# Decoder layer on one core: the softmax's division by its sum as a scaled copy on ScalarE instead of a product on VectorE

## The chip, the cores and the metric

The kernel runs on 1 core of one Trainium2 chip. The metric is the device time of one execution in microseconds (us); less is better. The core has five engines that run side by side and wait for one another through semaphores: TensorE (PE in the profile, its weight loads PEld), VectorE (DVE), ScalarE (ACT), GpSimd (POOL) and SyncE (SP, which issues the transfers).

## The reference

One decoder layer in float32 on x (8, 256, 128) and a context of the same shape. Each of its three parts adds its result to its input and normalises:

```python
x = _layernorm(x + attention(x, ...))
x = _layernorm(x + retention(x, ctx, ctx))
x = _layernorm(x + experts(x, ...))
```

The change touches the attention alone. For each query, an indexer picks 96 keys (the last 64, and 32 others that it rates highest); keys and values come from a latent of 32 numbers, with 8 heads:

```python
scores = (einsum("bhld,bhlkd->bhlk", q_c, k_c) + einsum("bhld,blkd->bhlk", q_r, key_r)) * scale
attn = softmax(scores, axis=-1)
out = einsum("bhlk,bhlkd->bhld", attn, v)
```

The softmax is exp(score - maximum), divided by the sum of these over the keys of a query and head. The retention part multiplies decayed scores with the context; the experts part takes the best two of 8 experts for every token.

## The kernel before

The program is one list of instructions for each engine, all written by one function `program`, so that every engine meets the pieces in the same order. The outer loop is over steps (one batch of 256 tokens starts its attention in each of the steps 0 to 7), the inner one over 20 slots of a step. Four strands of different batches are interleaved in a slot: `stage_a` (projections and the indexer's top keys, for the next batch), `stage_b` (attention, for this batch), `stage_c` (retention, for the batch before) and `stage_d` (router, two batches back). From step 2 on, `tile` adds the experts of earlier batches: four products with weights, four copies with a ReLU on ScalarE (`ht`, line 1581), four more products. The last third of a step's slots has no attention tile. After step 8 come the dense experts, without attention.

`stage_b` handles one tile of 16 tokens x 8 heads = 128 rows in each of the slots 0 to 15, 128 tiles in all. The first four tiles of a batch see 96 keys (the narrow form, 128x96), the other twelve see 96 near keys and 4 x 32 columns of gathered far ones (the wide form, 128x224). For tile t:

- PE, slot t: `scores` writes bank bS (lines 1088, 1091, 1094); `gather` fetches the far latents of the next tile into bG (line 1075).
- DVE, slot t: the maximum of a row, negated, into `nmx` (line 1808 narrow, line 1813 wide, where the scores also go to `pp`); then `gs` from bG (line 1820).
- ACT, slot t: `pp = exp(...)` with the sum of a row into `lsum` (line 1495, two instructions: the exponential and the read of the sum). At quarter past the slot it waits for PE's `turn` of the tile before and copies out `pts` (1505, 1507), `vgs` (1509), `ots` (1516).
- DVE, three quarters past: `rls = 1/lsum` (line 1798), then `ppn = pp * rls` (line 1801).
- PE, a quarter past slot t+1: `turn` transposes `ppn` into bank bM (line 919); in slot t+2 `weigh` multiplies it with the latents (lines 1117, 1122).

`pp`, `ppn`, `lsum`, `rls` and `nmx` have two buffers, by the parity of t. Signals count per tile: `s_exp` (exponential done), `s_rec` (reciprocal done), `s_nrm` (`ppn` written), `m_full` (bM filled), `m_out` (bM copied out). Three places wait for `s_nrm`: PE's `turn`, ACT's exponential and DVE's wide maximum, the last two for the tile two before theirs (their buffer of `pp`).

The order of the pieces within a slot, for every engine, is: stage_a, stage_c, stage_b at s; stage_d; the first half of an expert tile; stage_b at s+0.25; stage_a, stage_c, stage_d at s+0.5; stage_b at s+0.75; the second half of an expert tile.

Other lines that the prediction names: `sm` (line 1883, DVE, the retention's decayed scores, from PE's bC of line 1227), `qV` (line 1549, ACT, four copies scaled by a number of each partition), `kS` (line 1535, ACT, the same shape without that scale), `rb`, `pa`, `pr`, `ka` (stage_a's work on ACT), `oh` (line 1788), `xt` and `ot` (lines 2012, 2018, DVE, experts), the tile list (lines 1973 to 2000, DVE, once in each of three steps), `sorted_tokens` and `gb` (lines 863 and 851, POOL's indirect transfers), `taken` (line 1963, DVE, router).

Of the kernel before, what the change touches and what calls it, by code (L numbers as in the profile page):

```python
# [19 lines left out]
ALU = mybir.AluOpType  # L20
ACT = mybir.ActivationFunctionType
# [14 lines left out]
NT = L // TQ  # L36
# [186 lines left out]
def build(nc, io, out):  # L223
    ctx = ExitStack()
    with ctx:
# [1147 lines left out]

        @block.scalar
        def _(act):
            for s_ in (a_free, a_soft, own_aa, s_exp, m_out, c_freeA, c_ret, ln_rs, own_ac, r_ex, own_ad, f_rs):
                act.sem_inc(s_.sem, s_.per * s_.lead)
            AC = nc.scalar.activation
            copy = nc.scalar.copy
# [105 lines left out]
            def stage_b(s, i):  # L1485
                p = i.par
                if s < 0:
                    return
                if s == int(s):
                    if s < NT:  # L1490

                        act.wait_ge(s_max.sem, s_max.at(i.n, s + 1))
                        act.wait_ge(s_nrm.sem, s_nrm.at(i.n, s - 1))
                        w = 96 if s < T0 else SW
                        AC(pp[:, s % 2, 0:w], bS[:, 0:w] if s < T0 else pp[:, s % 2, :], ACT.Exp, scale=1.0 if s < T0 else -1.0,  # L1495
                           bias=nmx[:, s % 2:s % 2 + 1], accum_out=lsum[:, s % 2:s % 2 + 1]).then_inc(s_exp.sem, 1)
                    return
                if s > int(s) + 0.25:
                    return
                s = int(s)  # L1500
                if 1 <= s <= NT + 1:

                    act.wait_ge(m_full.sem, m_full.at(i.n, s))
                    if s <= T0:
                        last = copy(pts[0:96, 0:128], bM[0:96, 0:128])
                    elif s <= NT:
                        last = copy(pts[:, :], bM[:, 0:256])  # L1507
                    if T0 < s <= NT:
                        last = copy(vgs[:, :].rearrange("p (c l) -> p c l", c=4),
                                    bM[:, LATENT:LATENT + 128].rearrange("p (l c) -> p c l", c=4))  # L1510
                    if 2 <= s:
                        t = s - 2
                        if t == 0:

                            act.wait_ge(c_full.sem, c_full.at(i.n - 1, C_AT["out"] + 1))
                        last = copy(ots[:, :, TQ * t:TQ * t + TQ], bM[:, WEIGHED:WEIGHED + 32].rearrange("p (a q) -> p a q", a=2))
                    last.then_inc(m_out.sem, 1)
# [103 lines left out]

        @block.vector
        def _(dve):
            for s_ in (own_va, g_top, r_ks, r_qs, top_a, top_b, a_slot, o_ready, g_out, s_max, s_rec, s_nrm, c_freeV, ln_st, own_vc,
                       c_x1, c_x2, r_lg, r_m, r_place, own_vd, own_vf, f_st, ln_root):
                dve.sem_inc(s_.sem, s_.per * s_.lead)
            TT, TS, STT = nc.vector.tensor_tensor, nc.vector.tensor_scalar, nc.vector.scalar_tensor_tensor
# [147 lines left out]
            def stage_b(s, i):  # L1775
# [17 lines left out]
                if s == int(s) + 0.75 and s < NT:  # L1793

                    t = int(s)
                    w = 96 if t < T0 else SW
                    dve.wait_ge(s_exp.sem, s_exp.at(i.n, t + 1))
                    nc.vector.reciprocal(rls[:, t % 2:t % 2 + 1], lsum[:, t % 2:t % 2 + 1]).then_inc(s_rec.sem, 1)
                    dve.wait_ge(m_full.sem, m_full.at(i.n, max(0, t - 1)))
                    dve.wait_ge(s_rec.sem, s_rec.at(i.n, t + 1))  # L1800
                    TS(ppn[:, t % 2, 0:w], pp[:, t % 2, 0:w], rls[:, t % 2:t % 2 + 1], None,  # L1801
                       ALU.mult).then_inc(s_nrm.sem, 1)
                if s != int(s):
                    return
                if s < NT:
# [303 lines left out]
```

## Time and profile before

| | |
|---|---|
| median of 3 runs | 690.98 us (687.41 to 692.0) |
| the profiled execution | 683.81 us, its span 682.0 us |
| mean granted clock of TensorE | 0.906 |
| busy: PE, DVE, ACT, POOL | 578.3, 479.7, 362.2, 268.4 us |
| attention tiles | 128 (96 wide, 32 narrow), between 39 and 570 us |
| first maximum of the 8 batches, at | 39.6, 100.3, 163.2, 227.1, 297.7, 368.3, 446.6, 515.4 us |

The profile is of one execution, which was some 7 us under the median of the timed ones. Its instructions overlap: a DVE or ACT instruction often starts before the one ahead of it has ended, so that what an instruction costs its engine is the distance between starts, less than its duration. Idle time is put down to whoever released the engine last.

### The profile page before, as it was taken

The page shows a single profiled execution, that of the slowest core. Times are in us where ns is not written, and L with a number is a line of the kernel's source. Part 1 is how long each engine was busy: PE and PEld are TensorE (multiplying, and loading weights), DVE is VectorE, ACT ScalarE, POOL GpSimd, SP SyncE. Part 2 cuts the span into 40 slices and gives each one's busy share as a digit, 9 for nine tenths or more (in the row PEclk, how much of TensorE's full clock was granted, in tenths as well). Part 3 has the DMA queues.
Part 4 walks back from the last instruction along what each step waited for, and adds up shares of the span by engine and source line. Part 5 has one row for each costly group of instructions (what it writes and reads, how often), then busy time and mean ns, then how long its engine had stood idle before and what let it go on. Part 6 is the DMA issues. An engine that isn't in the chain of part 4 may idle for free.

```text
span 682.0 us, 22130 instructions
## 1 busy us (share of the span) xinstructions
PE 578.3 (85%) x8149; PEld 441.2 (65%) x8149; DVE 479.7 (70%) x1746; ACT 362.2 (53%) x1253; POOL 268.4 (39%) x428
## 2 busy tenths in 40 slices
PE   5379977996898789989997788979996998789996
PEld 4255654664566456776786566757885677678886
DVE  1948848986986798569965896679767685434653
ACT  4344545563655446637764554566654444554352
POOL 1415812911570287014801698418403563104310
PEclk9657797898899769989998799799998897999999
DMA  5030163113013142463335143543362524686551
GB/s 166 13 110 17 23 194 122 22 33 111 13 23 112 27 134 54 149 198 98 108 111 160 44 145 84 162 150 110 98 198 79 176 76 111 199 236 197 178 164 42
DMA packets 58594, 75.85 MB, mean 111 GB/s; under 512 B 14256, under 2 KB 47480, under 8 KB 57336
## 3 DMA queue, kind: packets, MB, share of 16 engines
q1 hardware_dynamic: 56952, 71.30, 35.1%
q0 software_dynamic: 1536, 3.15, 1.6%
q8 instruction: 65, 1.06, 0.7%
q14 instruction: 41, 0.34, 0.2%
HBM read 58.92 MB, written 8.62 MB: 99 GB/s over the span
## 4 chain that ended last, share of the span: by engine, by line
PE 31%; DVE 10%; POOL 10%; issue 8%; ACT 6%; DMA 1%; SPq 0%; DVEq 0%; POOLq 0%; ACTq 0%
PE bW L1352 4%; PE bH L1287 3%; PE bR L1302 3%; PE bG L1075 3%; POOL gb L851 3%; PE bM L919 2%; ACT qV L1549 2%; PE bH L1338 2%; PE bG L1338 2%; PE bS L1094 2%; PE bM L1122 1%; PE bM L1117 1%; ACT ht L1581 1%; POOL sorted_tokens L863 1%; PE bC L1227 1%
## 5 line engine op out<-in xcount | busy, mean ns | idle before, releaser
L1495 ACT ACTIVATE pp<-pp,nmx 128x224 f32<-128x224 f32 x96 | 46.5, 485 | 98.3 <-DVE nmx L1813 98.2
L1820 DVE TENSOR_TENSOR gs<-bG,rank_t 96x512 f32<-96x512 f32 x96 | 65.4, 681 | 11.8 <-PE bG L1075 11.6
L809 POOL TENSOR_TENSOR r<-x,cst 128x256 f32<-128x256 f32 x8 | 5.8, 726 | 145.3 <-DVE x L1847 145.3
L1075 PE MATMUL bG<-oh,kspl 128*96 128x512 f32 x160 | 59.4, 454 | 0.0
L1801 DVE TENSOR_SCALAR ppn<-pp,rls 128x224 f32<-128x224 f32 (+1 forms) x128 | 48.8, 382 | 14.5 <-PE bM L919 0.5
L1581 ACT ACTIVATE ht<-bH,wt 128x128 f32<-128x128 f32 x156 | 44.7, 375 | 22.1 <-PE bH L1287 22.1
L1883 DVE TENSOR_TENSOR sm<-bC,cst 128x512 f32<-128x512 f32 x64 | 43.4, 679 | 15.2 <-PE bC L1227 15.0
L919 PE MATMUL bM<-cst,ppn 128*128 128x128 f32 (+1 forms) x224 | 51.1, 300 | 3.2 <-DVE ppn L1801 3.2
L1227 PE MATMUL bC<-qV,kS 128*128 128x512 f32 x64 | 34.6, 540 | 17.3 <-DVE sm L1883 11.8
L1507 ACT COPY pts<-bM 128x256 f32<-128x256 f32 x96 | 35.0, 365 | 25.8 <-PE bM L919 25.3
L1302 PE MATMUL bR<-wt,ht 128*128 128x128 f32 x264 | 40.0, 300 | 9.4 <-DVE taken L1963 9.3
L1122 PE MATMUL bM<-pts,vgs 128*32 128x8 f32 x3072 | 46.7, 182 | 0.0
L1117 PEld LDWEIGHTS bM<-pts,ckw 96*32 96x32 f32 x1024 | 21.0, 112 | 38.9 <-issue 38.2
L1287 PE MATMUL bH<-xt,wt 128*128 128x128 f32 x312 | 44.5, 289 | 1.8 <-DVE xt L2012 1.8
L1302 PEld LDWEIGHTS bR<-wt,ht 128*128 128x128 f32 x264 | 37.0, 211 | 13.4 <-issue 11.0
L1094 PE MATMUL bS<-gs,qall 96*32 96x128 f32 x768 | 43.3, 300 | 2.0
L1091 PE MATMUL bS<-kd,qall 128*128 128x96 f32 x192 | 39.7, 291 | 6.1 <-DVE nmx L1813 6.0
L851 POOL DMA_INDIRECT gb<-expert_rows,slot x24 | 26.5, 1104 | 46.7 <-DMA expert_rows<-ot 40.2
L1813 DVE CUSTOM_DVE_ANT_0 pp<-bS,cst 128x224 f32<-128x224 f32 x96 | 36.3, 378 | 11.0 <-PE bS L1094 10.9
L1287 PEld LDWEIGHTS bH<-xt,wt 128*128 128x128 f32 x312 | 41.1, 203 | 2.6 <-DVE xt L2012 2.2
L1122 PEld LDWEIGHTS bM<-pts,vgs 128*32 128x32 f32 x3072 | 42.7, 119 | 0.0
L1091 PEld LDWEIGHTS bS<-kd,qall 128*128 128x128 f32 x192 | 33.8, 207 | 13.0 <-DVE nmx L1813 9.2
(294 smaller groups left out, 1583.8 us busy)
## 6 DMA issues: line engine op xcount, KB each, us to landing
wt<-in_experts SPq DMA_DIRECT2D x61, 578.0 KB, 4.1
sidx<-far_slots SPq DMA_DIRECT2D x8, 1536.0 KB, 6.8
vstk<-gs SPq DMA_DIRECT2D x96, 64.0 KB
xs<-sorted_tokens SPq DMA_DIRECT2D x45, 64.0 KB, 3.9
expert_rows<-ot SPq DMA_DIRECT2D x45, 64.0 KB, 3.6
sorted_tokens<-acc SPq DMA_DIRECT2D x9, 256.0 KB, 2.9
cst<-shape_constants SPq DMA_DIRECT2D x1, 1595.5 KB, 6.4
xn<-in_x SPq DMA_DIRECT2D x8, 128.0 KB, 3.2
```

The lines of the kernel that those rows point to most:

```text
L851: nc.gpsimd.indirect_dma_start(gb[:, n % NG, 2 * k + t, :], None, ys_dram[g][:, :], bass.IndirectOffsetOnAxis(ap=slot[:, n, 2 * k + t:2 * ...
L919: return MM(dst, src, ident[lo:lo + n, lo:lo + n], is_transpose=True, start=True, stop=True)
L1075: last = MM(w[0:96, :], table, oh[:, pair % 2, kt, SLOTS * (tile % 2):SLOTS * (tile % 2) + SLOTS], start=(n == 0), stop=(n == len(products ...
L1091: MM(bS[:, o:o + 96], q, kd[:, p, k0:k0 + 96], start=True, stop=True, skip_group_check=True)
L1094: last = MM(bS[32 * c:32 * c + 32, o + 96:o + SW], qall[0:96, p, 128 * tile + 32 * c:128 * tile + 32 * c + 32], gs[:, g % 2, 128 * c:128 * ...
L1122: last = MM(bM[32 * j:32 * j + 32, WEIGHED:WEIGHED + 32].rearrange("p (a q) -> p a q", a=2)[:, :, 4 * c:4 * c + 4], vgs[:, 32 * c:32 * c + ...
L1287: last = MM(w[:, 128 * f:128 * f + 128], wt[:, t % NW, 128 * f:128 * f + 128], xt[:, t % 2, :], start=True, stop=True)
L1302: last = MM(w[:, 0:128], ht[:, t % 2, f, :], wt[:, t % NW, W2_AT + 128 * f:W2_AT + 128 * f + 128], start=(f == 0), stop=(f == 3))
L1495: AC(pp[:, s % 2, 0:w], bS[:, 0:w] if s < T0 else pp[:, s % 2, :], ACT.Exp, scale=1.0 if s < T0 else -1.0, bias=nmx[:, s % 2:s % 2 + 1], a ...
L1581: last = AC(ht[:, t % 2, f, :], w[:, 128 * f:128 * f + 128], ACT.Relu, bias=wt[:, t % NW, FF + f:FF + f + 1])
L1801: TS(ppn[:, t % 2, 0:w], pp[:, t % 2, 0:w], rls[:, t % 2:t % 2 + 1], None, ALU.mult).then_inc(s_nrm.sem, 1)
L1820: TT(gs[:, g % 2, :].rearrange("p (t j) -> p t j", j=FAR), bG[0:96, :].rearrange("p (t j) -> p t j", j=FAR), rank_t[:, :].rearrange("p (o ...
```

## The change

The product `ppn = pp * rls` leaves VectorE. ScalarE computes it as a copy with the scale `rls` (one number for each partition), at s+0.75, which in ScalarE's order is behind its copies of the slot and behind what `stage_a` and `stage_c` do at s+0.5, and ahead of the experts' ReLU copies. The reciprocal stays on VectorE, and ScalarE waits for its signal `s_rec`. VectorE's own waits for `s_rec` and for `m_full` go away; ScalarE has waited for a later count of `m_full` at s+0.25.

```diff
@@ scalar engine, stage_b @@
+                if s == int(s) + 0.75 and s < NT:
+
+                    t = int(s)
+                    w = 96 if t < T0 else SW
+                    act.wait_ge(s_rec.sem, s_rec.at(i.n, t + 1))
+                    AC(ppn[:, t % 2, 0:w], pp[:, t % 2, 0:w], ACT.Copy, scale=rls[:, t % 2:t % 2 + 1]).then_inc(s_nrm.sem, 1)
@@ vector engine, stage_b @@
                     t = int(s)
-                    w = 96 if t < T0 else SW
                     dve.wait_ge(s_exp.sem, s_exp.at(i.n, t + 1))
                     nc.vector.reciprocal(rls[:, t % 2:t % 2 + 1], lsum[:, t % 2:t % 2 + 1]).then_inc(s_rec.sem, 1)
-                    dve.wait_ge(m_full.sem, m_full.at(i.n, max(0, t - 1)))
-                    dve.wait_ge(s_rec.sem, s_rec.at(i.n, t + 1))
-                    TS(ppn[:, t % 2, 0:w], pp[:, t % 2, 0:w], rls[:, t % 2:t % 2 + 1], None,
-                       ALU.mult).then_inc(s_nrm.sem, 1)
```

The two lists of signals that each engine raises once at its start are changed to match: `s_nrm` moves from VectorE's to ScalarE's.

## Rows read from the trace of the kernel before

**Rows 1.** The page: busy time; TensorE's clock in 40 slices (10 is full).
```profile
PE 578.3 (85%) x8149; PEld 441.2 (65%) x8149; DVE 479.7 (70%) x1746; ACT 362.2 (53%) x1253; POOL 268.4 (39%) x428
PEclk9657797898899769989998799799998897999999
```

**Rows 2.** Waits: engine, line, releaser, us in total, times, longest us.
```profile
ACT pp L1495 <- DVE nmx L1813: 98.2, 70, 3.3
ACT pp L1495 <- DVE nmx L1808: 39.7, 23, 3.0
...
PE bC L1227 <- DVE sm L1883: 11.8, 7, 3.4
...
PE bS L1091 <- DVE nmx L1813: 6.0, 8, 2.6
```

**Rows 3.** Lines by form: costs of removed, added and neighbouring instructions.
```profile
L1801 DVE TENSOR_SCALAR ppn<-pp,rls 128x224 f32<-128x224 f32 x96 | 38.1, 397 | 11.0 <-PE bM L919 0.5 <-DVE rls L1798 0.5
...
L1801 DVE TENSOR_SCALAR ppn<-pp,rls 128x96 f32<-128x96 f32 x32 | 10.7, 336 | 3.5
...
L1495 ACT ACTIVATE pp<-pp,nmx 128x224 f32<-128x224 f32 x96 | 46.5, 485 | 98.3 <-DVE nmx L1813 98.2
...
L1549 ACT ACTIVATE qV<-bC,cst 128x512 fp32r<-128x512 f32 x64 | 38.7, 691 | 2.1 <-PE bC L919 1.9
...
L1535 ACT CAST kS<-bC 128x512 fp32r<-128x512 f32 x16 | 9.6, 598 | 3.2 <-PE bC L919 3.2
```

**Rows 4.** Timeline of DVE in two slots of the third batch: start, duration.
```profile
179.42 0.16 DVE L1798 RECIPROCAL rls<-lsum 128x1 f32<-128x1 f32 x1
179.69 0.53 DVE L1801 TENSOR_SCALAR ppn<-pp,rls 128x224 f32<-128x224 f32 x1
180.13 0.08 DVE L1742 MATCH_VALUE_LOAD ia<-va,sa 128x8 f32 x1
...
183.41 0.15 DVE L1798 RECIPROCAL rls<-lsum 128x1 f32<-128x1 f32 x1
183.66 0.34 DVE L1801 TENSOR_SCALAR ppn<-pp,rls 128x224 f32<-128x224 f32 x1
183.92 0.29 DVE L1740 MAX8 va<-sa 128x8 f32<-128x128 f32 x1
```

**Rows 5.** Timeline of ACT, third and fifth batch.
```profile
163.44 0.34 ACT L1495 ACTIVATE pp<-bS,nmx 128x96 f32<-128x96 f32 x1 [1.50 <-DVE nmx L1808]
163.68 0.19 ACT L1495 ACTIVATION_READ_ACCUMULATOR pp<-bS,nmx 128x1 f32 x1
...
309.64 1.14 ACT L1581 ACTIVATE ht<-bH,wt 128x128 f32<-128x128 f32 x4
...
315.25 0.48 ACT L1495 ACTIVATE pp<-pp,nmx 128x224 f32<-128x224 f32 x1
315.64 0.19 ACT L1495 ACTIVATION_READ_ACCUMULATOR pp<-pp,nmx 128x1 f32 x1
```

**Rows 6.** Timeline of PE, third batch: idle before and releaser in brackets.
```profile
181.97 0.59 PE L1227 MATMUL bC<-qV,kS 128*128 128x512 f32 x1 [1.00 <-DVE sm L1883]
...
194.86 0.46 PE L1091 MATMUL bS<-kd,qall 128*128 128x96 f32 x2 [0.35 <-DVE nmx L1813]
...
201.05 0.44 PE L919 MATMUL bM<-cst,ppn 128*128 128x128 f32 x2 [0.91 <-DVE ppn L1801]
```

**Rows 7.** Chain that ended last, fourth batch: start, us, what.
```profile
231.90 0.27 DVE ppn L1801
...
258.33 0.69 DVE sm L1883
...
266.50 0.36 DVE ppn L1801
266.91 0.44 PE bM L919 x2
```

**Rows 8.** Windows of the fifth batch: busy us and instructions by engine.
```profile
core 0: us, PE busy (x) PEld busy (x) DVE busy (x) ACT busy (x) POOL busy (x), PEclk, DMA share, GB/s
...
327.00:357.00 30.00, 29.86 (x566) 23.98 (x567) 24.20 (x81) 18.61 (x65) 11.61 (x19) 1.00 0.40 111
```

**Rows 9.** Chain that ended last, sixth batch and start of the eighth.
```profile
379.24 1.03 POOL sorted_tokens L863
...
423.17 0.73 POOL acc L885
...
533.79 4.30 DMA expert_rows<-ot
```

More of the change, by code:

```diff
@@ L1375, in _ @@
         def _(act):
-            for s_ in (a_free, a_soft, own_aa, s_exp, m_out, c_freeA, c_ret, ln_rs, own_ac, r_ex, own_ad, f_rs):
+            for s_ in (a_free, a_soft, own_aa, s_exp, s_nrm, m_out, c_freeA, c_ret, ln_rs, own_ac, r_ex, own_ad, f_rs):
                 act.sem_inc(s_.sem, s_.per * s_.lead)
@@ L1623, in _ @@
         def _(dve):
-            for s_ in (own_va, g_top, r_ks, r_qs, top_a, top_b, a_slot, o_ready, g_out, s_max, s_rec, s_nrm, c_freeV, ln_st, own_vc,
+            for s_ in (own_va, g_top, r_ks, r_qs, top_a, top_b, a_slot, o_ready, g_out, s_max, s_rec, c_freeV, ln_st, own_vc,
                        c_x1, c_x2, r_lg, r_m, r_place, own_vd, own_vf, f_st, ln_root):
```

## The prediction

> **What bounds the kernel now.** I read the page's busy times first [rows 1]. TensorE leads with 85%, VectorE has 70%, ScalarE 53%. The row of clocks shows that the first half of the attention runs partly at half clock. No engine is full over the whole span, so a share tells little. The reader should ask of every stretch which engine sets the pace.
>
> The list of waits came next [rows 2]. ScalarE's exponential waits for VectorE's maximum in 70 of the 96 wide tiles and in 23 of the 32 narrow ones, 137.9 us in all, 1.5 us each time. ScalarE is normally ahead and VectorE late. But TensorE waits little for VectorE: 11.8 us for `sm`, 6.0 us for the maximum. These two, with single waits for `ppn`, are what a quicker VectorE can give back during the tiles.
>
> The chain that ended last and the timelines then tell how a batch goes. It has three kinds of stretch. In some VectorE is the pace (around 181, 195 and 200 us [rows 6], around 231 and from 258 to 266 us [rows 7]). In some ScalarE has no pause (309.6 to 315.6 us, where the copies of the experts and of stage_a stand one behind the other [rows 5]). In the rest it is TensorE: from 327 to 357 us it is busy for 29.86 of 30 us [rows 8]. In the sixth batch and in the middle of the eighth the chain runs through POOL's indirect transfers [rows 9].
>
> **The change, part by part.**
>
> *Removed from VectorE.* The product takes 397 ns wide and 336 ns narrow, 48.8 us in all [rows 3]. What it costs the engine is a distance of starts. At 183.41 the reciprocal starts, at 183.92 what follows the product; less the reciprocal's own 0.15 us that is 0.36 us [rows 4]. The distance also holds the gap of 0.10 us in which VectorE waits for its own reciprocal. At 179.42 it was 0.71 - 0.16 = 0.55 us, since the product took 0.53 us there. I take 0.38 us wide and 0.30 us narrow (its product, 336 ns on average, is some 60 ns shorter): 96 x 0.38 + 32 x 0.30 = 46 us come free on VectorE. The wait for `m_full` stopped it once (0.5 us) [rows 3] and is worth nothing.
>
> The Trainium skill ("SBUF — State Buffer", who interferes with whom) says that a Vector product with a scalar can hold the port pair that Vector and GpSimd share, for the whole instruction, and that ScalarE has ports of its own. The 0.53 us against 0.34 us [rows 4] agree with such a lock. By it the freed 46 us would be nearer the upper figure, 0.55 us, where GpSimd works; the sum below doesn't use it.
>
> *Added to ScalarE.* The trace has no copy of this shape from SBUF with a scale of each partition. From above the exponential of the same shape, which reads one number of each partition and also adds up, bounds it: 485 ns [rows 3]. Its read of the sum starts 0.39 us behind it wide (315.25 to 315.64) and 0.24 us narrow [rows 5]. From below: the scale alone makes `qV` 93 ns longer than `kS` at 512 columns [rows 3], so at the least 0.1 us. The exponential is nearest in shape, source and operands, so I take 0.39 and 0.24 us: 96 x 0.39 + 32 x 0.24 = 45 us more on ScalarE, which then is busy for some 60% of the span.
>
> *The new wait.* ScalarE now stands at s+0.75 until VectorE's reciprocal of this tile. Queued behind it are the experts' ReLU copies and the next slot's copies and exponential. The exponential needs the next maximum, which VectorE computes behind that very reciprocal, so the wait itself costs it nothing; only the 0.39 us of the copy can. VectorE's next maximum takes at least as long as that after the reciprocal. The copy is hidden in the 93 tiles in which ScalarE waits today, by 1.5 us on average [rows 2]. Its cover is gone in the other 35: 26 x 0.39 + 9 x 0.24 = 12 us, if ScalarE were the pace in all of them. TensorE's `turn` needs `ppn` one slot later. Where it waits for it, the time from the reciprocal's end stays about the same: 0.10 + 0.34 us before, a signal to the other engine and some 0.4 us after.
>
> *Where the 46 us go.* I followed the shift through the batches.
>
> First three batches (no experts beside them). In the third, the slots up to 178 us gain on VectorE and lose it again in ScalarE's row of copies. Then three stalls of TensorE are within reach [rows 6]: the 1.00 us at 181.97, of which one wide product, 0.38 us, goes; the 0.35 us at 194.86, all of it; and the 0.91 us at 201.05, of which two more slots of VectorE would give 0.76 us and TensorE, now earlier itself, lets through some 0.6 us. That is 1.3 us. The other two have the same order of work: 3 x 1.3 = 3.9 us.
>
> Fourth batch. Two narrow slots on the chain around 231 us give 0.6 us, and three wide ones from 258 to 266 us [rows 7] 1.1 us; 1.7 us.
>
> Fifth and seventh. They open with the experts' copies in ScalarE's row [rows 5]. One narrow slot gives 0.3 us, two copies on ScalarE's path take 0.5 us, one wide slot gives 0.4 us, and from 327 us on TensorE is full [rows 8] and nothing counts. 0.1 us each.
>
> Sixth and eighth. Two narrow slots ahead of POOL's stretch [rows 9] give 0.6 us each; what comes within it is swallowed. 1.3 us for these four batches with rounding. The dense end has no attention and gives nothing.
>
> The sum is 3.9 + 1.7 + 1.3 = 6.9 us. The profiled execution of 683.81 us (span 682.0, 1.8 us around it) would become 676.9 us. The median of the runs lies 7.2 us above that execution, for reasons that the trace can't show; I set the forecast against the median: 690.98 - 6.9, about 684 us.
>
> **The rivals.**
>
> *A. Nothing arrives.* TensorE, its clock and POOL set the pace nearly everywhere, and what is gained in VectorE's stretches is lost a few us later, as in the fifth batch. For it: seven eighths of the freed 46 us are dead already by my own count. Against it: the stalls of [rows 6] are real. The time would be 688 to 693 us.
>
> *B. ScalarE becomes the pace; this one ends slower.* The copy stands ahead of the experts' ReLU copies and of `qV`, on which TensorE waits. The mechanism is ScalarE's row of copies between two exponentials; the price is the 12 us of the 35 uncovered tiles, with none of the 6.9 us earned, so up to 703 us. It decides as soon as ScalarE's copies are the last to arrive in more than some 18 wide tiles (18 x 0.39 = 7 us). Against it: ScalarE's mean wait of 1.5 us. The Trainium skill ("ScalarE: Activation LUTs", rules for kernel authors) tells authors to multiply on VectorE and not on ScalarE; here the instruction's own cost is indeed no less on ScalarE (0.39 against 0.38 us), so by that rule only the idle time speaks for the move.
>
> *C. More comes back than stalls.* TensorE stands at half clock behind pauses in which it waited for VectorE [rows 1]; with shorter pauses a stretch of some 8 us of half clock, which costs 4 us, may fall away in two or three batches. Also VectorE's products of 0.5 us beside GpSimd go. 684 less 8 to 12 us is 672 to 676 us. It can as well go the other way by one stretch.
>
> That the change doesn't do what it says (the instruction splits in two, or loads a table) would show as a second ScalarE instruction; a copy with a scale stands in this kernel as `qV` without one.
>
> **How the numbers follow.** A difference under 1% (7 us) can't be told from none in this kernel, whose own runs spread over 687 to 692 us. Chances: forecast 0.50 (gain of 3 to 11 us, somewhat more than half of it over 1%), A 0.22, B 0.14, C 0.14. Faster by over 1%: 0.14 + 0.5 x 0.56 = 0.42. Within 1%: 0.22 + 0.22 = 0.44. Slower by over 1%: 0.14. The range leaves out the upper part of B and the lower of C: 674 to 695 us.
>
> **What the profile after would show.** Line 1801 gone and a ScalarE group of 128 copies, 450 to 480 ns wide; VectorE near 430 us busy, ScalarE near 415. ScalarE's wait for the maximum should fall from 138 us to about 100, and a new wait for the reciprocal should appear. TensorE's waits for `sm`, the maximum and `ppn` should fall by some 5 us in the first four batches, and its busy time should stay. If instead TensorE waits longer for `pr`, `qV` or `ht`, B is at work. The forecast is wrong if the copy costs over 0.5 us from start to start, or if the clock's row changes more than the waits do.

## The result, and the profile after

| | before | after |
|---|---|---|
| median of 5 runs | 690.98 us (686.59 to 692.0) | 669.88 us (669.39 to 672.18) |
| ratio, 95% interval | | 0.9734 (0.9699 to 0.977) |
| profiled execution, its span | 683.81, 682.0 us | 671.91, 670.1 us |

The kernel became 2.7% faster, 18.4 us of the 690.98 by the ratio. The forecast was 684 us, a gain of 6.9; the time lies under its range. The direction was right, the size too small by a factor of 2.7. The two profiled executions differ by only 11.9 us, because the one of before was 7 us under its median.

The page of the kernel after, which answers to [rows 1]:

```profile
PE 569.7 (85%) x8149; PEld 437.9 (65%) x8149; DVE 433.0 (65%) x1618; ACT 407.6 (61%) x1381; POOL 265.1 (40%) x428
PEclk9757797998899789979997799889999899999999
```

VectorE loses 128 instructions and 46.7 us, ScalarE gains 128 and 45.4 us; 46 and 45 were forecast. TensorE has the same 8149 instructions and is busy 8.6 us less; its mean granted clock rose from 0.906 to 0.919 of 2.4 GHz.

The copy by form, kernel after (count | us in all, mean ns | idle before it, and whose signal ended it):

```profile
L1503 ACT ACTIVATE ppn<-pp,rls 128x224 f32<-128x224 f32 x96 | 47.0, 489 | 30.3 <-DVE rls L1803 29.4 <-issue 0.5
L1503 ACT ACTIVATE ppn<-pp,rls 128x96 f32<-128x96 f32 x32 | 11.9, 373 | 3.6 <-DVE rls L1803 3.5
```

It lasts 489 ns; the exponential from which it was bounded lasts 485 [rows 3]. The waits of the kernel after (us, times, longest), which answer to [rows 2]:

```profile
ACT ppn L1503 <- DVE rls L1803: 32.9, 63, 1.5
ACT pp L1495 <- DVE nmx L1809: 30.1, 24, 2.4
ACT pp L1495 <- DVE nmx L1814: 29.3, 32, 1.6
DVE pp L1814 <- PE bS L1094: 25.5, 31, 1.9
DVE sm L1884 <- PE bC L1227: 23.7, 26, 4.4
...
PE bC L1227 <- DVE sm L1884: 8.3, 7, 2.3
...
PE bS L1091 <- DVE nmx L1814: 3.8, 2, 3.3
```

Read them as a shift of who waits for whom. ScalarE's wait for the maximum falls from 137.9 to 59.4 us. A new one for the reciprocal takes 32.9, and the copies themselves take up 45 of what is left. VectorE waits more for TensorE's banks: 49 us in the two rows shown, where the same two had 10.9 and 15.0 us. TensorE's own waits for `sm` and the maximum fall from 17.8 to 12.1 us, which is the "some 5 us" of the prediction. These waits alone would have given the forecast. The rest has to be found elsewhere.

**Where it came back, by batch.** The start of a batch is the start of its first maximum in VectorE's timeline. The table has the mean distance between starts. The product's five profiles are the one of before, e0, e1, e2 and whichever of e4 and e5 has the product in that batch; the copy's four are the one of after, e3, e12 and the other of e4 and e5 (the experiments are described below).

| batch | product on VectorE, us | copy on ScalarE, us | gain | predicted |
|---|---|---|---|---|
| 1 | 60.6 | 59.0 | 1.6 | 1.3 |
| 2 | 63.5 | 60.5 | 2.9 | 1.3 |
| 3 | 63.2 | 60.6 | 2.6 | 1.3 |
| 4 | 72.2 | 69.2 | 3.0 | 1.7 |
| 5 | 70.1 | 69.9 | 0.1 | 0.1 |
| 6 | 81.4 (78.3 to 87.4) | 77.8 (77.6 to 78.2) | 3.6 | 0.6 |
| 7 | 69.8 | 69.6 | 0.3 | 0.1 |
| 8, its slots; and the end behind them | | | 1.6 and 1.9 | 0.6 and 0 |

Fifth and seventh came as forecast. The second to fourth bring about twice as much, the sixth six times. Single profiles of one kind differ by 0.2 to 3.7 us in a batch (by 9 us in the sixth with the product), so the second and third batch, where even the closest pair of product and copy differs by 2.2 and 1.0 us, are the safest rows. The first batch's 1.6 us hangs on one profile (e4, 56.96 us); without it the gain is 0.9. The 1.9 us at the end lie within the spread of single profiles (112.1 to 116.3 us with the product, 111.8 to 113.2 with the copy) and stay unexplained.

**Where within a batch.** Windows cut at the starts of the maxima show every slot by itself. The third batch of the kernel before, in its second profile (e0), in which TensorE's clock was full in slots 3 to 14 (shown are slots 1, 4 to 6, 8 to 11, 14, 15; window, length, then the busy us of PE, PEld, DVE, ACT, POOL with their instructions, and the granted clock):

```profile
168.91:171.87 2.96, 2.19 (x17) 1.56 (x19) 2.71 (x11) 0.75 (x4) 0.00 (x0) 0.50 0.00 0
...
180.42:183.68 3.26, 2.43 (x24) 1.27 (x23) 3.11 (x15) 0.95 (x5) 2.88 (x9) 1.00 0.10 20
183.68:187.46 3.78, 2.80 (x57) 1.82 (x57) 3.67 (x16) 1.09 (x5) 3.70 (x5) 1.00 0.08 17
187.46:190.64 3.18, 3.05 (x74) 2.17 (x78) 3.03 (x13) 2.76 (x10) 3.02 (x6) 1.00 0.13 28
...
195.37:197.79 2.42, 1.85 (x51) 1.10 (x52) 2.31 (x9) 1.09 (x5) 2.34 (x5) 1.00 0.05 8
197.79:201.84 4.05, 3.87 (x85) 2.88 (x74) 3.94 (x12) 2.16 (x6) 3.78 (x6) 1.00 0.15 34
201.84:203.85 2.01, 1.87 (x17) 1.07 (x15) 1.90 (x7) 1.59 (x6) 1.73 (x4) 1.00 0.00 0
203.85:207.64 3.79, 3.79 (x94) 2.91 (x93) 2.81 (x8) 2.91 (x8) 0.61 (x4) 1.00 0.23 42
...
214.61:216.24 1.63, 1.56 (x51) 1.18 (x40) 1.48 (x6) 1.20 (x6) 0.00 (x0) 1.00 0.08 19
216.24:229.45 13.21, 10.33 (x171) 8.90 (x171) 7.08 (x37) 5.03 (x18) 0.12 (x1) 0.74 0.52 163
```

The same slots of the changed kernel, run again beside the last experiments (e12):

```profile
164.65:167.22 2.57, 1.80 (x15) 1.26 (x17) 2.43 (x9) 1.11 (x5) 0.00 (x0) 0.50 0.00 0
...
176.06:179.16 3.10, 2.46 (x33) 1.43 (x32) 2.82 (x13) 1.92 (x10) 2.17 (x8) 1.00 0.10 21
179.16:182.87 3.71, 3.02 (x57) 1.85 (x57) 3.71 (x14) 1.57 (x6) 3.55 (x6) 1.00 0.09 18
182.87:185.46 2.59, 2.46 (x47) 1.91 (x48) 2.55 (x13) 2.17 (x9) 2.43 (x5) 1.00 0.12 25
...
189.93:191.83 1.90, 1.76 (x16) 0.94 (x14) 1.90 (x9) 1.31 (x6) 1.82 (x4) 1.00 0.00 0
191.83:194.97 3.14, 3.14 (x76) 2.25 (x79) 3.14 (x11) 1.60 (x7) 3.00 (x5) 1.00 0.24 50
194.97:197.31 2.34, 2.34 (x59) 1.93 (x52) 1.65 (x6) 2.34 (x8) 2.13 (x6) 1.00 0.03 5
197.31:201.45 4.14, 4.14 (x95) 3.11 (x94) 2.47 (x9) 3.54 (x10) 1.80 (x6) 1.00 0.19 36
...
207.59:209.78 2.19, 2.15 (x61) 1.50 (x60) 1.18 (x6) 1.75 (x7) 0.00 (x0) 1.00 0.15 30
209.78:221.24 11.46, 8.19 (x171) 6.82 (x171) 6.66 (x35) 5.61 (x20) 0.12 (x1) 1.00 0.60 187
```

VectorE is busy for over nine tenths of slots 1 and 3 to 10 of before, and of 13 and 14. Seven of these shrink clearly: slots 1, 4, 6, 7, 8, 9 and 13, by 0.39, 0.16, 0.59, 0.26, 0.52, 0.91 and 0.38 us. Slot 3, in which ScalarE is full too, and slot 5 stay nearly as they were (0.04 us longer and 0.07 shorter). Where TensorE or ScalarE is full (slots 10, 11, 14) part comes back: 0.33, 0.35 and 0.56 us, and 0.25 us in slot 2; slot 12, in which TensorE is full as well, shrinks by 0.45. Over slots 0 to 14 the sum is 51.05 against 48.85 us, a gain of 2.2. The profile of e1, which has VectorE's product at full clock from slot 3 on, gives 51.04 us for the same slots. Slot 15 adds 1.75 in this pair, because the clock of before was 0.74 in it and 1.00 after; that isn't the change's doing, for e3 and e6, with the copy, show 0.74 there as well. The second batch gives 2.4 us by the same sum (51.60 against 49.17), and slots 1, 2 and 8 of the fourth and the sixth batch are shorter by 0.38 to 0.53 us each.

Why slot 5 gave next to nothing is seen in VectorE's timeline, first e0, then e12. An instruction ahead of the place of the product took 0.37 us longer:

```profile
184.58 0.74 DVE L1788 TENSOR_SCALAR oh<-sidx,cst 128x1024 fp32r<-128x1024 bf16 x1
```

```profile
180.07 1.11 DVE L1794 TENSOR_SCALAR oh<-sidx,cst 128x1024 fp32r<-128x1024 bf16 x1
```

What one tile costs VectorE is read in slot 9. The kernel before (e0):

```profile
200.62 0.14 DVE L1798 RECIPROCAL rls<-lsum 128x1 f32<-128x1 f32 x1
200.87 0.34 DVE L1801 TENSOR_SCALAR ppn<-pp,rls 128x224 f32<-128x224 f32 x1
201.12 0.17 DVE L1767 CAST ja<-ia 128x32 bf16<-128x32 uint32 x1
201.21 0.71 DVE L1769 CAST jb<-ib 64x32 bf16<-64x32 uint32 x1
```

and after (e12):

```profile
194.66 0.15 DVE L1803 RECIPROCAL rls<-lsum 128x1 f32<-128x1 f32 x1
194.73 0.23 DVE L1773 CAST ja<-ia 128x32 bf16<-128x32 uint32 x1
194.88 0.16 DVE L1775 CAST jb<-ib 64x32 bf16<-64x32 uint32 x1
```

From the reciprocal to what follows it is 0.50 us before and 0.07 after: 0.43 us a wide tile, not 0.38. Over the tiles behind which VectorE has no pause the medians say the same: 0.52 us in the profile of before and 0.07 after in wide tiles, 0.46 and 0.07 in narrow ones. With nobody waiting for it at once, the reciprocal itself is nearly free to VectorE. The cast `jb` behind it took 0.71 us here and 0.16 after, and from its start to the maximum it was 0.63 against 0.09 us. These two, less 0.06 us from one cast to the next, make the 0.91 us of slot 9.

### The profile page after: what moved, and what is told of

Same layout as the page of the kernel before. It is cut to its first block, busy times and chain, and to the rows that moved or that the text cites. A ratio compares the mean times of both kernels' runs of the same rounds, so it can differ in the third digit from the quotient of the medians.

```text
span 670.1 us, 22002 instructions
## 1 busy us (share of the span) xinstructions
PE 569.7 (85%) x8149; PEld 437.9 (65%) x8149; DVE 433.0 (65%) x1618; ACT 407.6 (61%) x1381; POOL 265.1 (40%) x428
## 4 chain that ended last, share of the span: by engine, by line
PE 34%; POOL 10%; ACT 8%; issue 7%; DVE 6%; DMA 1%; SPq 0%; DVEq 0%; POOLq 0%; ACTq 0%
PE bW L1352 4%; PE bR L1302 4%; PE bH L1287 3%; PE bG L1075 3%; POOL gb L851 3%; PE bM L919 3%; ACT qV L1555 2%; PE bH L1338 2%; PE bG L1338 2%; ACT ht L1587 2%; PE bS L1094 2%; PE bM L1122 1%; PE bM L1117 1%; POOL sorted_tokens L863 1%; PE bC L1227 1%
## 5 line engine op out<-in xcount | busy, mean ns | idle before, releaser
L1503 ACT ACTIVATE ppn<-pp,rls 128x224 f32<-128x224 f32 (+1 forms) x128 | 58.9, 460 | 33.9 <-DVE rls L1803 32.9
L742 POOL TENSOR_TENSOR ktab<-kr,ka 128x64 f32<-128x64 f32 x8 | 2.6, 321 | 103.6 <-ACT ka L1469 80.8
L851 POOL DMA_INDIRECT gb<-expert_rows,slot x24 | 25.0, 1041 | 45.4 <-DMA expert_rows<-ot 38.9
L1091 PE MATMUL bS<-kd,qall 128*128 128x96 f32 x192 | 38.0, 281 | 4.0 <-DVE nmx L1814 3.8
```

The source lines that it names most:

```text
L851: nc.gpsimd.indirect_dma_start(gb[:, n % NG, 2 * k + t, :], None, ys_dram[g][:, :], bass.IndirectOffsetOnAxis(ap=slot[:, n, 2 * k + t:2 * ...
L1503: AC(ppn[:, t % 2, 0:w], pp[:, t % 2, 0:w], ACT.Copy, scale=rls[:, t % 2:t % 2 + 1]).then_inc(s_nrm.sem, 1)
```

## The experiments

The variants ran in four sets (e0 to e3, e4 to e7, e8 to e11, e12 to e14). All ratios are to the kernel before, run beside them on the same chip. In three of the sets the kernel before took 707 us and not 691, and every variant moved with it (see the last section); in the set of e4 to e7 it took 689.

**e0: the kernel before once more.**

> The kernel before, unchanged, profiled once more. Its one profiled execution was 7 us under its median. Theory T (time on VectorE ahead of TensorE's short stalls, and the half-clock stretches that follow them): the time stays within 0.5% of before, and this profile differs from the first one, if at all, in where TensorE runs at half clock, by 3 to 8 us in the span. Rival: the profiles agree slot by slot, and the 7 us lie outside what a trace shows.

Measured: 708.02 us against 706.87, ratio 1.0017 (0.9978 to 1.0056). With some ten runs differences down to 0.4% can be told. The two profiles differ by 24.4 us, more than either expectation had, and 15 us of it lie in the eighth batch (last section); the rest is spread over the others, up to 3 us in one. Neither expectation describes that.

**e1: the copy on ScalarE, and the product on VectorE as well.** The changed kernel, with VectorE's product written to a buffer that nobody reads:

```diff
                     nc.vector.reciprocal(...).then_inc(s_rec.sem, 1)
+                    w = 96 if t < T0 else SW
+                    dve.wait_ge(s_rec.sem, s_rec.at(i.n, t + 1))
+                    TS(spare[:, t % 2, 0:w], pp[:, t % 2, 0:w], rls[:, t % 2:t % 2 + 1], None, ALU.mult)
```

> The changed kernel, with VectorE computing the same product as before into a spare buffer that nobody reads, at its old place and with its old wait for the reciprocal; ppn still comes from ScalarE. Theory T (VectorE's time is what counts): VectorE has its 46 us back and the gain goes, 686 to 694 us. Rival (the gain comes from an earlier or otherwise placed ppn on ScalarE): it stays at 670 to 675 us.

Measured: 707.87 us, ratio 1.0006 (0.9971 to 1.0041). The whole gain is gone, as theory T expected. It comes from VectorE's time (the product and its wait for the reciprocal together) and from nothing else in the change: not from the wait for `m_full` that went, nor from where `ppn` is made.

**e2: the reverse.** The kernel before, with a copy on ScalarE at s+0.75 into the spare buffer, behind the same wait for the reciprocal:

```diff
+                if s == int(s) + 0.75 and s < NT:
+                    ...
+                    act.wait_ge(s_rec.sem, s_rec.at(i.n, t + 1))
+                    AC(spare[:, t % 2, 0:w], pp[:, t % 2, 0:w], ACT.Copy, scale=rls[:, t % 2:t % 2 + 1])
```

> The kernel before, with ScalarE's copy added at its new place, into a spare buffer that nobody reads; ppn still comes from VectorE. It prices ScalarE's copy alone. Theory T with a price for ScalarE's copies in the batches that carry experts: 2 to 5 us slower than before, 692 to 696 us. Rival (ScalarE has room everywhere): the same as before within 1 us.

Measured: 705.08 us, ratio 1.0002 (0.9965 to 1.0039). ScalarE's 128 copies and their wait cost nothing, to within 0.4%, which is 2.6 us. Of the expected 2 to 5 us only the lower end fits; the rival (ScalarE has room) is the better reading. In the trace of e2 ScalarE waits 34.5 us for the reciprocal:

```profile
ACT spare L1504 <- DVE rls L1805: 34.5, 64, 1.6
```

and its waits for the maximum are 42.8 and 31.7 us, where they were 137.9: the copy and the new wait lie within the old one.

**e3: a short copy.** The changed kernel, with ScalarE's copy over 16 columns (the rest of `ppn` keeps a constant that is written once at the start):

```diff
-                    AC(ppn[:, t % 2, 0:w], pp[:, t % 2, 0:w], ACT.Copy, ...)
+                    AC(ppn[:, t % 2, 0:16], pp[:, t % 2, 0:16], ACT.Copy, ...)
```

> The changed kernel with ScalarE's copy cut to 16 of its 96 or 224 columns (the rest of ppn keeps a constant set at the start, so the division is left out for them). ScalarE gets back some 0.17 us a wide tile and 0.07 us a narrow one, about 18 us of the 45. Theory T: 1 to 4 us faster than the changed kernel, mostly in the fifth and the seventh batch, where the profile after shows it slower than before by 1.0 and 1.6 us. Rival (the copy is hidden everywhere): within 1 us of the changed kernel.

Measured: 689.09 us against 706.87, ratio 0.973 (0.9685 to 0.9775). The copy lasts 308 ns (median) in place of 489, and no gain beyond the change's own (0.9734, and 0.972 in e12) is seen. The interval is 3 us to either side, so the time can't tell the expected 1 to 4 us from the rival's none. The fifth and the seventh batch, where the gain was looked for, took 69.3 and 70.1 us in its profile, against 69.4 and 68.9 in e12.

**e4 and e5: the change in half the batches**, the first four or the last four:

```diff
-                if s == int(s) + 0.75 and s < NT:
+                if s == int(s) + 0.75 and s < NT and (i.n < 4):
```

(e5: `i.n >= 4`; VectorE keeps the product in the other batches.)

> The change for the first four batches only; the last four keep VectorE's product. The profiles put 8.9 us of gain by the start of the fifth batch and 3.0 us behind it, with losses in the fifth and seventh. Theory T: 674 to 680 us, some three quarters of the gain. By the prediction's own sum (5.6 of 6.9 us in these batches): 685 us.

> The change for the last four batches only. Theory T: 684 to 689 us, since the fifth and the seventh batch lose on ScalarE what the others gain. By the prediction's own sum: 689.7 us. Rival (the gain is spread evenly over the tiles): 680 us, as for the first half.

Measured: 0.98 (0.97 to 0.9901) and 0.9873 (0.9792 to 0.9954); 675.58 and 680.57 us against 689.07. By these the first half brings 13.8 us and the second 8.8, each known to some 6 or 7 us; their sum agrees with the 18.4 of the whole within that. The prediction had 5.6 and 1.3. e4 came where theory T expected it. e5 didn't: 684 to 689 us were expected, and it took the 680 of the rival, an even spread over the tiles. The two intervals overlap, so these runs don't say how uneven the spread is.

**e6: tiles 2 and 3 of each batch stay on VectorE.** In the third batch ScalarE is full for much of slots 2 and 3 ("loses it again in ScalarE's row of copies"):

> The changed kernel, but tiles 2 and 3 of each batch keep VectorE's product: there ScalarE's copies (qV, the experts', stage_a's) stand without a pause. Theory T: 0.2 to 0.5 us a batch back, 1 to 4 us faster than the changed kernel, 666 to 669 us. Rival (VectorE is the pace there as well): the same or up to 4 us slower.

Measured: 670.38 us, ratio 0.9725 (0.9641 to 0.981), the ratio of the change. The interval is 6 us to either side, wider than the 1 to 4 us at stake, so e6 decides neither for theory T nor for its rival. Better evidence for the prediction's reading of these slots is in the windows: slots 0 to 3 of the third batch take 15.23 us in e0 and 15.13 in e12.

**e7: the copy behind the next tile's exponential**, so that ScalarE never stops for the reciprocal:

```diff
                            bias=nmx[...], accum_out=lsum[...]).then_inc(s_exp.sem, 1)
+                    if 1 <= s <= NT:
+                        t = s - 1
+                        ...
+                        act.wait_ge(m_full.sem, m_full.at(i.n, max(0, t - 1)))
+                        act.wait_ge(s_rec.sem, s_rec.at(i.n, t + 1))
+                        AC(ppn[:, t % 2, 0:w], ...).then_inc(s_nrm.sem, 1)
                     return
-                if s == int(s) + 0.75 and s < NT:
-                    ...
```

> The changed kernel with ScalarE's copy of tile t moved behind the exponential of tile t+1, ahead of the copies of that slot: it never holds up an exponential, and ScalarE never waits for the reciprocal, but TensorE's turn gets ppn later. Theory T: ppn was early enough in most tiles, so the same as the changed kernel within 3 us. Rival (TensorE's turn stands right behind ppn): 4 to 15 us slower, with TensorE waiting for ppn in most tiles.

Measured: 743.08 us against 689.07, ratio 1.0767 (1.0675 to 1.086). That is some 72 us above the changed kernel: the same within 3 us was expected, 4 to 15 us slower by the rival, and both are far off. TensorE's two queues now wait for `ppn`:

```profile
PEld bM L919 <- ACT ppn L1502: 87.4, 74, 4.0
PE bM L919 <- ACT ppn L1502: 73.4, 63, 3.8
```

In the kernel after, TensorE's wait for it is 3.4 us in all. The 0.5 us copy is harmless only because it stands before the next exponential; behind it `ppn` is a whole maximum and exponential later, and `turn` is in the middle of TensorE's order. ScalarE in turn waits 83 us for the bank that `turn` fills, at its copy `pts`, where it is 34 us in the kernel after.

**e8: a dose.** The kernel before, with VectorE's product over 16 columns (the rest of `ppn` a constant, as in e3). It lasts 291 ns where it was 397 and 336, and VectorE is busy 467.4 us in its profile, 12.3 less than the kernel before, where the change takes off 46.7:

> The kernel before with VectorE's product cut to 16 columns (the rest of ppn keeps a constant, so the division is left out for them); its waits for the reciprocal and for m_full stay. It frees the length of the product, some 0.15 us narrow and 0.2 to 0.3 us wide, of the 0.30 and 0.38 us. Theory T (time on VectorE, whatever it is made of): about half to two thirds of the gain, ratio 0.980 to 0.988. Rival (the wait for its own reciprocal is what counts): ratio above 0.99.

Measured: 701.78 us against 707.29, ratio 0.9948 (0.9901 to 0.9995). Theory T had expected 0.980 to 0.988 and missed; the time is on the rival's side. One reason is that the short product frees less than the expected 0.2 to 0.3 us: from the reciprocal to what follows, the median of a wide tile falls from 0.52 to 0.41 us. A quarter of the time brings a fifth of the gain (0.5 of 2.7%), 0.3 us for each us, where the change has 0.4. That fits a gain in proportion to VectorE's time, but the interval (0.4 to 7 us) holds nearly no gain as well. It doesn't exclude that the wait for its own reciprocal, which e8 keeps, is worth more than its share.

**e9, e10, e11: spare products against the half clock.** Rival C of the prediction says that what a late VectorE costs is in good part TensorE at 1.2 GHz behind its pauses. To fill the pauses, TensorE gets products of 96 columns into bank bG that nobody reads:

```diff
+            def keep_busy(n):
+                for _ in range(n):
+                    MM(bG[:, 0:96], ident, ident[:, 0:96], start=True, stop=True, skip_group_check=True)
+            EXTRA = {17: 4, 18: 4, 19: 4, 1: 8, 2: 12}
...
+                keep_busy(EXTRA.get(s, 0))
```

e9 is the kernel before with these 32 a batch, e10 the changed one with the same, e11 the changed one with 64.

> The kernel before with 32 spare products on TensorE for each batch (4 each at the start of slots 17, 18, 19, 8 at slot 1, 12 at slot 2), written to a bank that nobody reads then, where TensorE stands idle for 0.5 to 1.5 us before a half-clock stretch. Theory C (each pause of TensorE drags several us of half clock behind it, and part of the change's gain is that clock): the granted clock rises from 0.90 to 0.94 or more, and the time falls by 1 to 2% in spite of the added work. Rival (the clock follows and costs nothing, TensorE waits for others anyway): the time is the same or up to 1% longer, by 256 products of about 0.1 us.

> The changed kernel with the same 32 spare products for each batch. Theory C: another 1 to 2% off the changed kernel, ratio to before 0.955 to 0.965. Rival: ratio 0.973 to 0.98, as the changed kernel or a little slower.

> The changed kernel with 64 spare products for each batch (6, 8, 8, 8 at slots 16 to 19, 8, 10, 16 at slots 0 to 2). Theory C: the clock rises further, but the added work of some 7 us a batch begins to stand on the path; within 1% of the run with 32. Rival (clock without price): 1 to 3% slower than the run with 32.

Measured, against 707.29: 1.0299 (1.0227 to 1.0371), 1.0053 (1.0019 to 1.0087) and 1.0632 (1.0576 to 1.0689). The mean clock over the runs rises (0.896 without, 0.920 in e9, 0.938 in e10, 0.951 in e11), and the time rises as well. Neither expectation held for any of the three. This was a poor test: each product is two instructions, and in e9 the 256 products keep TensorE busy for 67.8 us, 8.5 us of a batch. That the kernels were slower is most likely the products' own time. One thing can be read all the same: with the same spare products in both, the changed kernel is 16.2 us faster (0.978).

**e12, e13, e14: spare products that fit.** Ten a batch, `EXTRA = {1: 4, 2: 6}`, where TensorE has idle time before slots 1 and 2. e12 is the changed kernel again, e13 the kernel before with the ten, e14 the changed one with the ten.

> The changed kernel once more, beside the next two on the same chip. Expected by every theory: a ratio of 0.970 to 0.977 to the kernel before.

> The kernel before with spare products on TensorE where it has idle time: four in slot 1 and six in slot 2 of each batch (96 columns, into the bank bG, read by nobody; 0.22 us each by the earlier run, so 0.9 and 1.3 us a slot). Theory C (stretches at half clock behind TensorE's pauses are an important part of what a slow VectorE costs): with the pauses filled, less half clock than 93 us and a ratio under 1, 0.990 to 0.997. The rival (the clock follows but brings little; the pauses themselves and VectorE's arrears are what counts): 1.000 to 1.008, since the products cost something where they don't fit.

> The changed kernel with the same ten spare products in each batch. Theory C: the distance between the two kernels shrinks, since both have their pauses filled; a ratio to the run above of 0.980 or more. The rival: the distance stays at 0.973 within 0.005.

Measured, against 707.22:

| | us | ratio | mean clock of the runs |
|---|---|---|---|
| before | 707.22 | | 0.896 |
| e12, changed | 688.68 | 0.972 (0.9671 to 0.9768) | 0.913 |
| e13, before with ten | 711.28 | 1.0067 (1.0034 to 1.0099) | 0.912 |
| e14, changed with ten | 694.54 | 0.98 (0.9743 to 0.9857) | 0.926 |

e13 has the clock of e12 and is 22.6 us slower. The distance between e13 and e14 is 16.7 us (0.976), against 18.5 without the products. Rival C expected 0.980 or more; its opposite, that the distance stays, is what came, though the uncertainty of each ratio (0.003 and 0.006) includes 0.98. The 4 us that e13 is above the kernel before were within its rival's range. They mix the clock with the products' own time: in the first batch e13's slot 0 takes 1.7 us longer than e0's. In the second and third batch the ten products cost nothing (slots 1 and 2 take 2.97 and 4.40 us in e13 and 2.96 and 4.40 in e0). e12, then e13, then e14 (columns as above):

```profile
100.30:160.90 60.60, 50.39 (x870) 34.74 (x870) 44.60 (x166) 40.26 (x138) 23.84 (x45) 0.94 0.31 95
160.90:221.20 60.30, 50.76 (x870) 35.01 (x870) 44.67 (x166) 40.22 (x138) 23.75 (x45) 0.94 0.18 50
```

```profile
102.70:165.70 63.00, 52.95 (x893) 36.85 (x893) 50.31 (x182) 34.35 (x122) 24.62 (x45) 0.97 0.29 89
165.70:229.60 63.90, 54.34 (x893) 37.59 (x891) 50.88 (x182) 34.41 (x122) 24.49 (x45) 0.95 0.18 47
```

```profile
100.90:161.50 60.60, 52.35 (x893) 37.02 (x894) 44.60 (x166) 40.12 (x138) 24.45 (x45) 0.97 0.29 95
161.50:221.20 59.70, 50.84 (x892) 35.76 (x892) 44.57 (x166) 39.90 (x138) 23.72 (x45) 1.00 0.18 50
```

With VectorE's product, at a clock of 0.97 and 0.95, the two batches take 63.0 and 63.9 us. With ScalarE's copy they take 60.6 and 60.3 us at the lower clock of 0.94, and 60.6 and 59.7 at 0.97 and 1.00. Slots 1 and 2 of the third batch stood at a clock of 0.50 and 0.67 in e0 and at 1.00 in e13 and took the same time, so with the product the lower clock costs nothing there; with the copy slot 2 took 4.65 us at 0.54 and 4.40 at 1.00.

The mean clock of a batch hides one thing. The ten products raise the clock chiefly in slots 0 to 2, where they stand. In e13's third batch slots 5 and 6 still stand at 0.64 and 0.53, and slot 6 takes 4.40 us, where e0 has 3.18 at full clock:

```profile
187.99:192.39 4.40, 4.40 (x50) 3.09 (x49) 3.38 (x13) 2.58 (x9) 4.24 (x8) 0.53 0.08 17
```

So of the 3.6 us between e13 and e12 in the third batch 1.2 are the clock's; the 2.4 us of the second batch and the 2.2 us of e0 against e12 are VectorE's.

## Why the prediction was wrong in size

**Right.** What VectorE is given (46 us forecast, 46.7 less busy) and what ScalarE is charged (45 against 45.4). That the new wait costs nothing and that the copy is hidden: e2 shows it to within 2.6 us, and e3 agrees. Rival B, ScalarE as the pace, had 0.14 and is out by e2. The Trainium skill's advice to multiply on VectorE rather than ScalarE ("ScalarE: Activation LUTs", rules for kernel authors), which stood beside it, goes by the time of the instruction: here the ScalarE instruction is the longer one (489 against 397 ns) and the kernel is 2.7% faster with it. Right, too, were slots 0 to 3 of the third batch (15.23 us before, 15.13 after), and the near nothing of the fifth and seventh batch. The direction was argued from stalls that are real; that rival C's time came was in part luck (below).

**The step that failed** is the sum under "Where the 46 us go", in its terms for the first four batches, the sixth and the eighth: 3.9 for the first three, 1.7, 0.6 and 0.6. The batches brought 7.1, 3.0, 3.6 and 1.6, with 1.9 more behind the last slots. The rule behind the first three was "three stalls of TensorE are within reach": a gain was taken for real only where TensorE's timeline showed idle time released by VectorE, and capped by that idle time. The fourth batch's term counted the slots that one chain happened to pass. The runs show another count. VectorE sets the pace also where no stall of TensorE names it. In slot 6, which lost 0.59 us, TensorE was busy for 3.05 of 3.18 us, and in slot 1, which lost 0.39, its one stall is put down to ScalarE, which had itself waited 2.74 us for VectorE's maximum (e0; the same row stands in e12 with the same 1.69 us, so the gain never shows in it):

```profile
169.68 0.74 PE L1088 MATMUL bS<-kd,qall 128*128 128x96 f32 x2 [1.69 <-ACT pp L1495]
```

Slots cut at VectorE's maxima show the gain directly. In the third batch that is 2.2 us at nearly equal clock, where 1.3 was forecast. Two smaller faults of the sum: by its own words the fifth and seventh batch have 0.3 - 0.5 + 0.4 = 0.2 us each and not 0.1, and the four late batches then 1.6 and not 1.3; and the reciprocal's own 0.15 us was taken off what comes free, though the next instruction starts 0.07 us behind the reciprocal's start. By the medians above 96 x 0.45 + 32 x 0.38, some 55 us, came free and not 46. Together these would have added 1 to 2 us to the 6.9.

**Term by term in the third batch.** The stall at 181.97 was given 0.38 us: slot 4 brought 0.16 in the pair shown and 0.47 in the first pair of profiles. The one at 194.86 was given 0.35: slot 8 brought 0.52, all of VectorE's relief there. The one at 201.05 was given 0.6: slots 9 to 11 together 0.91 - 0.33 - 0.35 = 0.23, since TensorE and ScalarE are full behind it, as the prediction feared. In the first pair of profiles, from which the 0.6 was read, these three slots gave 10.18 against 9.65 us, so that this term was about right there. Not counted at all were slots 6, 7, 12 and 13, 1.68 us together, from which slot 14 takes back 0.56.

**The eighth and sixth batch.** "What comes within it is swallowed" was said of POOL's stretch and is too strong. The sixth batch took 78.3 to 87.4 us with the product and 77.6 to 78.2 with the copy; in three of the five profiles with the product it was over 81 us. Against the two short ones the copy gains some 0.5 us, near the forecast's 0.6. Whether the change keeps the long ones out isn't shown: with the copy and spare products they come too (e14 80.8, e10 81.8 us). Why they happen is open.

**Rival C** named the time, 672 to 676 us; by the ratio it became 672.6. Its mechanism was not found as the main cause, so that its time is in part luck. Stretches of half clock do fall away: at the same place of the third batch before and after (the first pair of profiles) have

```profile
181.00:191.00 10.00, 9.03 (x147) 6.38 (x148) 8.86 (x32) 4.57 (x16) 9.53 (x15) 0.66 0.08 18
```

```profile
178.50:188.50 10.00, 8.08 (x162) 5.42 (x162) 9.04 (x33) 6.36 (x22) 9.53 (x16) 1.00 0.11 22
```

This place is slots 5 and 6. In the second and third batches of the profiles of the table it is below full clock in seven of ten with the product and in one of eight with the copy. From the times of slot 6 at full and at lower clock (3.45 and up to 4.34 us in the second batch with the product) I estimate that this brings 0.3 to 0.4 us of the mean gain of each of these two batches. That is rival C's mechanism, but far below the 4 us that it counted for a batch. e13 raises the mean clock of the kernel before to that of the changed one and wins nothing, but it leaves the half clock of this place as it is, so it isn't the clean test of C that it was meant to be. The prediction said it would be wrong "if the clock's row changes more than the waits do", and in the first pair of profiles that is the case: TensorE's busy time fell by 8.6 us, its idle time by only 3.3. That sign was misleading, since a TensorE that is late for VectorE's sake can spend the time idle at full clock or busy at half clock, and the trace books the two differently. What share of the 18.4 us is the clock's stays open. In the second and third batch the slot sums at about equal clock (2.4 and 2.2 us) leave 0.4 to 0.5 us of the mean gains of 2.9 and 2.6 for it, which agrees with the estimate above; for the other batches nothing separates it.

**Point by point of what the profile should show.** Line 1801 gone, 128 copies of 489 ns wide (450 to 480 forecast): yes, a little longer. VectorE 433 busy (430), ScalarE 407.6 (415): yes. ScalarE's wait for the maximum near 100 us: it fell to 59.4, but with the reciprocal's wait it is 92.3, so the forecast had the sum and not the split. TensorE's waits for `sm`, the maximum and `ppn` together 21.0 us before and 15.5 after: the forecast 5. Its busy time "should stay": it fell by 8.6.

**The reference point.** The forecast was set against the median and the sum was read from an execution 7 us faster. In that profile the fourth and the sixth batch were some 3 us shorter than in e0; they are two of the batches that the sum had too small. A single profile at the fast end of its kernel can hide part of what its lateness costs; that it did so here isn't shown.

## What to carry to other kernels

When an engine that is not the busiest one paces some of the slots, cut its timeline at one instruction of each slot and ask of every slot which engine is full in it. The relief can count in every slot in which that engine is full and no other is, also where no stall of the busiest engine carries its name, and a part of it is taken back where another engine is full. It isn't certain in each: slot 5 above, with VectorE busy for 3.67 of 3.78 us, gave 0.07 of 0.43. Work can move for nothing to an engine that stands waiting for the donor's next result, if it stands ahead of that wait: the same copy behind the next exponential (e7) cost 7.7%, where here it gained 2.7%. A change of the granted clock beside a change of the waits is not yet a cause; compare the same slots at equal clock, since a mean over a batch can hide the one slot that matters.

## What the runs showed of the hardware that was not expected

A pause of TensorE with no releaser. In three of the four sets every kernel, changed or not, has a slot of some 13.3 to 14.3 us in the middle of the eighth batch, which was 2.6 us in the first profile. TensorE's timeline there, kernel before once more:

```profile
550.62 1.84 PE L1210 MATMUL bR<-sm,cnm 128*32 128x128 f32 x11
553.25 0.68 PE L1210 MATMUL bR<-sm,cnm 128*32 128x128 f32 x5 [0.79 <-issue]
554.71 0.66 PE L1210 MATMUL bR<-sm,cnm 128*32 128x128 f32 x5 [0.77 <-issue]
```

The 32 products of line 1210 come in groups of mostly five with 0.8 to 1.0 us between them, in which TensorE waits for nothing that the profile shows. The window of that slot has a granted clock of 0.50, 1.2 GHz throughout:

```profile
548.90:562.50 13.60, 9.12 (x91) 4.54 (x91) 1.53 (x6) 2.45 (x8) 11.14 (x12) 0.50 0.42 115
```

Elsewhere the same 32 stand in one row of 1.08 us (kernel after, at 183.42 us). Most of the step from 691 to 707 us is this place. It follows the set of runs, not the kernel, and one chip showed both levels. In all eleven profiles that have it, POOL's indirect reads of `gb` (line 851) run beside these 32 products, six or seven of the eight, and slot 4 of that batch takes 7.1 to 7.5 us. In the six that don't, slot 4 takes 2.8 to 4.8 us, the products stand before these reads (in e7 beside the first one), and they last 1.08 us. In the sixth batch, though, one or two such reads run beside the same products in several profiles, which last 1.08 us there in nearly all. So the meeting goes with the pause, but no run shows it as the cause. The pause doesn't touch the ratios: 0.9734 at the one level, 0.972 at the other.

VectorE beside POOL. `oh` (128x1024) takes 0.74 us as a rule and up to 1.14 in some slots (e0), and the small cast `jb` took 0.71 us in one place and 0.16 in another, in slots in which POOL is busy. The Trainium skill ("SBUF — State Buffer", who interferes with whom) has Vector and GpSimd share a port pair that one of them can hold; these rows agree with it, and no run here separates it from other causes. It can fall either way for the change: in slot 9 it gave 0.54 us, in slot 5 it took 0.37.
